# All 71 matmuls on constants that stand in TensorE's pauses are taken out of a two-block conv and FFN kernel

## The chip, the cores and the metric

One core of one Trainium2 chip. The metric is the device time of one execution in microseconds (us), the median of several runs. The hardware profiler gives one execution's trace besides: what each engine ran and when, and the clock that TensorE was granted.

## The reference, cut to what matters

The input is x, 4 images of 32 channels and 28 x 28 points. Four blocks with a residual follow one another. The norm ahead of each, `ln_c` or `ln_t`, is over the 32 channels of a point, since the tokens are the points.

```python
x = x + L0_conv(ln_c(x))          # 1x1 conv, L1-distance conv (adder2d) 1x1, BN, relu,
                                  # 3x3 conv, adder2d 3x3, BN, relu, + identity, relu
t = to_tokens(x)                  # (4, 784, 32)
t = t + L0_ffn(ln_t(t), ...)      # scan over 33 steps, see below
x = from_tokens(t, x)
x = x + L1_conv(ln_c(x), ...)     # two 3x3 convs with quantised weights and activations
t = to_tokens(x)
t = t + L1_ffn(ln_t(t), ...)      # causal convolution with 16 filters, mixed by 32x32 matrices
x = from_tokens(t, x)

def step(h, p):                   # L0_ffn, scanned over 33 sets of weights
    op = argmax(h[0, 0, :19])     # the first token chooses one of 19 operations
    y = softmax(q k^T * scale) v @ p['wo'][op]      # q, k, v = h @ p['wq'][op], ...
    h = where(p['am'][op], y, h)  # attention only where the mask says so
    z = relu(h @ p['w1'][op] + p['b1'][op]) @ p['w2'][op] + p['b2'][op]
    h = where(p['fm'][op], z, h)
    return h, None
```

## The kernel before

Each engine has its own instruction stream, written out by hand, and they meet by semaphores alone. Partitions hold 4 images x 32 channels, the 784 points lie along the free dimension, in halves of 392 (`half`) or quarters of 196 (`quarter`). Everything is float32 except the quantised convs. A float32 matmul call shows in the trace as two matmul instructions, each with its weight load. All of TensorE's matmuls go through the helper `mm`, so they carry one line, L879, and are told apart by the tiles they read.

The order of the work on TensorE:

1. `norm(0)`: the mean over channels of each point by a matmul of X with the constant `bones` (two halves, on tiles X,CON), DVE subtracts it, ACT squares, a matmul with `vsel` sums the squares (TMP,CON), ACT takes the root (SDC), DVE the reciprocal (RSC), and `spread` (four calls, RSC,CON) copies the result to all channels; DVE multiplies. The same `norm` runs four times (k = 0 to 3).
2. 1x1 conv (XN,WS), the correction with `CORRN` (QZ,CORRN), and 8 adder groups. In an adder group ACT or DVE makes one plane of |x - w| or max(x, w) of the whole batch (L338, L365, L534, L729), and TensorE sums it over channels in 8 calls (`group`, pool_,CON).
3. 3x3 conv (H1P,WS) and 72 more adder groups; `norm(1)`.
4. The scan. `token_row` brings the first token's row to partition 0; DVE finds the operation and the next step whose mask is set (`decide`), writes it to KINT (semaphore `decided`), and every engine reads it and jumps in three nested loops (`active_steps`). SP fetches the step's weights, DVE lays them out in blocks (W1B, W4B), and then attention (projection H,W4B; scores QZ,Y; `weigh` multiplies the exponentials with VT and with ones) and FFN (H,W1B, then W2S) run where the step asks for them. With this input two steps run: the first has FFN alone, the second attention and FFN. Then the row is read a third time, nothing is left, and all engines leave the loops.
5. `norm(2)`, two quantised 3x3 convs (H1P,CQ, bf16), `norm(3)`, short matmuls with shifted copies (CW,MUB and CON,CW), and the filter bank: 64 `filtered` and 16 `mixed` blocks on HE and pool_, dense up to the end.

Between these stand calls of `keep_warm(n)`: n matmuls of constants with constants (CON with itself, 128 x 196 columns; in `inputs` the tile XC, part of TMP, which DVE has just set to zero) into a PSUM bank that nobody reads at that point. The numbers are in `WARM`. They stand: `inputs` ahead of everything; `means` in each norm after the two mean matmuls; `deviations` in each norm after vsel; `choice` after each token row; `weights` at the head of each step; `exponentials` before the last image's four `weigh`; `sums` before the wait for the last of the weighed sums. Nothing waits for them.

Of the kernel before, what the change touches and what calls it, by code (L numbers as in the profile page):

```python
# [22 lines left out]
P = 128  # L23
NIMG, C, SIDE = 4, 32, 28
T = SIDE * SIDE
QU = T // 4
# [4 lines left out]
NB, NOPS, HID = 33, 19, 128  # L31
STEPS = (3, 4, 3)

WARM = dict(inputs=4, means=1, deviations=4, choice=8, weights=8, exponentials=5, sums=2)
OPW = 1024
QT, NQ = 112, 7
NK = 16
# [31 lines left out]
@contextmanager  # L69
def active_steps(e, code):  # L70


    assert STEPS[0] * STEPS[1] * STEPS[2] >= NB
    with e.Fori(0, STEPS[0]):
        with e.If(e.snap(code, min_val=0, max_val=4 * NB + 7) > 0):
            with e.Fori(0, STEPS[1]):
                with e.If(e.snap(code, min_val=0, max_val=4 * NB + 7) > 0):
                    with e.Fori(0, STEPS[2]):
                        c = e.snap(code, min_val=0, max_val=4 * NB + 7)
                        with e.If(c > 0):  # L80
                            yield c
                        e.nop()
                e.nop()
        e.nop()


def build(nc, x, par, con, ws1, wa1c, wa1r, ws2, wa2c, wa2r, amt, fmt, fwa, fwb, aw,
          cw1, cw2, phe, pho, mpp, mpm, mu, out):
    with ExitStack() as ctx:
# [11 lines left out]
        XC, SQ, SD, RS = (TMP[:, n * T:n * T + T] for n in range(4))  # L101
# [46 lines left out]
        def con_(name, w=None, rows=P):  # L148
            a = CC[name]
            return CON[0:rows, a:a + (w or P)]  # L150
# [4 lines left out]
        def half(ap, h):  # L155
            return ap[:, h * HT:(h + 1) * HT]

        def quarter(ap, q):
            return ap[:, q * QU:(q + 1) * QU]
# [6 lines left out]
        def bank(b, w=HT, rows_=slice(0, P)):  # L166
            return PS[rows_, b, 0:w]
# [709 lines left out]
        def _(t):  # L877
            def mm(out_, lhsT, rhs, start=True, stop=True):
                return t.matmul(out_, lhsT, rhs, start=start, stop=stop, skip_group_check=True)  # L879

            def keep_warm(n, src=CON, b=3):

                for _ in range(n):
                    mm(bank(b, QU), src[:, 0:P], src[:, 0:QU])

            def spread(h, to):

                for q in (2 * h, 2 * h + 1):
                    last = mm(PS[:, to + h, QU * (q % 2):QU * (q % 2) + QU], con_("spread", 512)[:, P * q:P * q + P], RSC[:, :])
                return last  # L890

            def norm(k, src, ready=None):
                for h in range(2):
                    if k == 0:
                        t.wait_ge(s["x_low_in" if h else "x_in"], 16)
                    if ready:
                        t.wait_ge(s[ready], h + 1)
                    mm(bank(h), con_("bones"), half(src, h)).then_inc(s["ln_mean"], 1)
                keep_warm(WARM["means"])
                for q in range(4):  # L900
                    t.wait_ge(s["ln_sq"], 2 * k + q // 2 + 1)
                    last = mm(PS[32 * q:32 * q + 32, 2, 0:QU], con_("vsel", C), quarter(SQ, q))
                last.then_inc(s["ln_var"], 1)
                keep_warm(WARM["deviations"])
                t.wait_ge(s["ln_rs"], k + 1)
                for h in range(2):
                    spread(h, 0).then_inc(s["ln_bc"], 1)

            t.wait_ge(s["idle_src"], 1)
            keep_warm(WARM["inputs"], XC)  # L910
            t.wait_ge(s["con_head"], 16)
            norm(0, X)
            t.wait_ge(s["ws_rep"], 1)
            for h in range(2):
# [52 lines left out]
            for h in range(2):  # L967
                last = mm(bank(6 + h), con_("ident"), half(XS9, h), False, False)
            last.then_inc(s["adder_done"], 1)
            norm(1, X1, "x1_ready")  # L970
            t.wait_ge(s["ln_out"], 4)

            def token_row():
                mm(PS[0:1, 6, 0:32], H[:, 0:1], con_("ident", 32)).then_inc(s["row_done"], 1)
                keep_warm(WARM["choice"])

            token_row()
            t.wait_ge(s["decided"], 1)
            code = t.alloc_register("t_code"); na = t.alloc_register("t_na"); nf = t.alloc_register("t_nf")
# [3 lines left out]
            chosen = t.alloc_register("t_chosen")  # L983
            t.reg_mov(chosen, 1)
            with active_steps(t, code) as c:
                keep_warm(WARM["weights"])
                with t.If((c & 1) > 0):
                    k = t.snap(na, min_val=0, max_val=NB)
                    t.wait_ge(s["zeroed"], 4)
# [44 lines left out]
                    def weigh(b, pair):  # L1034

                        t.wait_ge(s["exp_done"], k * 28 + (NQ * b + min(2 * pair + 2, NQ)))
                        if pair == 0:
                            if b:
                                t.wait_ge(s["ae_done"], k * 4 + b)
                            else:  # L1040
                                t.wait_ge(s["v_done"], k + 1)
                        for h in range(2):
                            for w in range(2):
                                for e in range(2):
                                    j = 2 * pair + e
                                    if j < NQ:
                                        q = 64 * w + 32 * e
                                        last = mm(PS[q:q + 32, 6 + h, 0:HT],
                                                  con_("ones", C, QT) if w else VT[0:QT, j, 32 * b:32 * b + 32],
                                                  half(SCR[0:QT, NQ * (b % 2) + j, :], h), pair == 0, j + 2 >= NQ)  # L1050
                        last.then_inc(s["pv_done"], 1)
# [16 lines left out]
                    weigh(NIMG - 2, 2)  # L1068
                    maxima_spread(NIMG - 1)
                    weigh(NIMG - 2, 3)  # L1070
                    keep_warm(WARM["exponentials"], b=0)
                    for pair in range(4):
                        weigh(NIMG - 1, pair)
                    t.wait_ge(s["wo_diag"], k + 1)
                    keep_warm(WARM["sums"], b=0)
                    t.wait_ge(s["ae_done"], k * 4 + 4)
                    for b in range(NIMG):
                        for q in range(4):
# [12 lines left out]
                with t.If((c & 2) > 0):  # L1091
# [18 lines left out]
                    t.wait_ge(s["ffn_h"], k * 2 + 2)  # L1110
                    t.reg_add(nf, nf, 1)
                token_row()
                n = t.snap(chosen, min_val=1, max_val=NB)
                t.wait_ge(s["decided"], n + 1)
# [4 lines left out]
            n = t.snap(chosen, min_val=1, max_val=NB + 1)  # L1119
            t.wait_ge(s["x2_ready"], n)  # L1120
            norm(2, X)
            t.wait_ge(s["cq_done"], 2)
            for i, (w, src) in enumerate(((CQ1, XQP), (CQ2, HQP))):
# [177 lines left out]
```

## Time and profile before

| | |
|---|---|
| median of 3 runs | 438.93 us (436.95 to 442.23) |
| the profiled execution | 438.08 us, span of its instructions 436.3 us |
| mean granted clock of TensorE | 0.98 of full speed |
| TensorE matmuls busy | 395.4 us, 91%, 4974 instructions |
| DVE busy | 244.8 us, 56% |
| ACT busy | 185.9 us, 43% |
| GpSimd busy | 17.3 us, 4% |

The span is from the first to the last instruction; the execution's time is 1.8 us longer. Matmuls are pipelined and their ends are modelled, so a group of n matmuls lasts about (n - 1) starts' spacing and one latency. "Issue" is idle time of an engine in which it waited for nothing that the profile shows, for example while its sequencer jumps. The granted clock is in shares of 2.4 GHz; 0.50 is 1.2 GHz.

### The profile page before, as it was taken

The numbers are of one execution on the slowest core, as the hardware profiler recorded it, in microseconds if no ns is written. First come the engines' busy times: TensorE is split into PE (matmuls) and PEld (weight loads), VectorE is DVE, ScalarE is ACT, GpSimd is POOL, SyncE is SP. The second block draws the span as 40 slices with busy tenths as digits, with TensorE's granted clock in tenths as the row PEclk, the third lists the DMA queues.
The fourth block names the chain that finished last, engine by engine and source line by source line (L and its number), as shares of the span: only waits on it lengthen the run. The fifth ranks groups of instructions, "written<-read, shape, count | busy, mean of one in ns | idle before, by whom it ended". The sixth has DMA issues, their size and how long they took to land.

```text
span 436.3 us, 11302 instructions
## 1 busy us (share of the span) xinstructions
PE 395.4 (91%) x4974; PEld 228.1 (52%) x4974; DVE 244.8 (56%) x337; ACT 185.9 (43%) x179; POOL 17.3 (4%) x30
## 2 busy tenths in 40 slices
PE   6899999999999898799989889866799999999996
PEld 4436357633333374656353534434377666777774
DVE  1797899999999455565747495434621121212121
ACT  2554888878787113144737366322221111111110
POOL 3054000000000200000000000000000000000000
PEclk9899999999999989999999999998989999999999
DMA  4139000000000250000000000000000000000001
GB/s 141 23 82 374 27 2 2 2 3 2 2 2 2 86 213 10 15 0 0 2 0 2 0 2 2 0 2 0 0 2 2 3 3 5 4 3 3 3 3 40
DMA packets 9768, 11.58 MB, mean 27 GB/s; under 512 B 3894, under 2 KB 8888, under 8 KB 9720
## 3 DMA queue, kind: packets, MB, share of 16 engines
q1 hardware_dynamic: 9352, 9.55, 6.7%
q0 software_dynamic: 224, 1.10, 0.8%
q8 instruction: 41, 0.67, 0.6%
q10 hardware_dynamic: 144, 0.20, 0.1%
q14 instruction: 7, 0.06, 0.0%
HBM read 10.44 MB, written 0.40 MB: 25 GB/s over the span
## 4 chain that ended last, share of the span: by engine, by line
PE 72%; DVE 14%; issue 6%; ACT 3%; DMA 2%; SPq 1%; DVEq 1%; ACTq 0%
PE PS L879 72%; DVE pool_ L788 3%; DVE pool_ L729 3%; DVE TMP L800 1%; ACT pool_ L393 1%; DMA PAR<-in_par 1%; DVE RSC L497 1%; ACT pool_ L409 1%; DMA W4R<-in_aw 1%; SPq L212 1%; ACT TMP L397 0%; DVE TMP L842 0%; DVE TMP L843 0%; DVE CW L686 0%; DVE SMX L805 0%
## 5 line engine op out<-in xcount | busy, mean ns | idle before, releaser
L879 PE MATMUL PS<-pool_,CON 128*32 128x392 f32 (+1 forms) x1392 | 132.3, 497 | 1.1 <-DVE pool_ L729 1.0
L879 PEld LDWEIGHTS PS<-pool_,CON 128*32 128x32 f32 (+1 forms) x1392 | 54.2, 111 | 60.2 <-issue 45.1
L365 ACT ACTIVATE pool_<-TMP,WA 128x3136 f32<-128x3136 f32 x27 | 78.5, 2929 | 16.6 <-PE PS L879 16.3
L729 DVE TENSOR_SCALAR pool_<-TMP,WA 128x3136 f32<-128x3136 f32 x45 | 82.0, 1847 | 0.2
L868 DVE COPY pool_<-PS 128x392 f32<-128x392 f32 x32 | 18.1, 566 | 84.0 <-PE PS L879 84.0
L463 ACT ACTIVATE pool_<-PS 128x392 f32<-128x392 f32 x32 | 15.9, 497 | 85.8 <-PE PS L879 85.8
L879 PE MATMUL PS<-pool_,WS 128*32 128x136 f32 (+3 forms) x1024 | 46.3, 333 | 0.0
L879 PE MATMUL PS<-HE,WS 128*32 128x136 f32 (+3 forms) x1024 | 46.3, 333 | 0.0
L879 PEld LDWEIGHTS PS<-pool_,WS 128*32 128x32 f32 x1024 | 32.0, 110 | 14.8 <-issue 9.8
L879 PEld LDWEIGHTS PS<-HE,WS 128*32 128x32 f32 x1024 | 31.5, 111 | 15.5 <-issue 11.2
L879 PE MATMUL PS<-QZ,Y 128*112 128x392 f32 x112 | 39.4, 498 | 0.0
L393 ACT ACTIVATE pool_<-pool_ 112x784 f32<-112x784 f32 x28 | 23.3, 853 | 17.2 <-DVE pool_ L788 17.2
L409 ACT ACTIVATE pool_<-PS 112x784 f32<-112x784 f32 x28 | 22.8, 814 | 16.4 <-PE PS L879 16.4
L879 PE MATMUL PS<-pool_,VT 112*32 112x392 f32 x112 | 23.9, 498 | 6.3 <-ACT pool_ L393 6.2
L788 DVE TENSOR_TENSOR pool_<-pool_,PS 112x784 f32<-112x784 f32 x28 | 26.5, 964 | 5.2 <-PE PS L879 5.2
L879 PE MATMUL PS<-CON 128*128 128x196 f32 x136 | 28.1, 354 | 0.2 <-issue 0.2
L879 PEld LDWEIGHTS PS<-QZ,Y 128*112 128x112 f32 x112 | 18.6, 176 | 17.0 <-issue 12.9
L879 PEld LDWEIGHTS PS<-CON 128*128 128x128 f32 x136 | 24.1, 202 | 6.3 <-issue 5.7
L800 DVE TENSOR_TENSOR TMP<-TMP,pool_ 112x784 f32<-112x784 f32 x20 | 19.5, 973 | 5.7 <-ACT pool_ L409 5.7
L879 PE MATMUL PS<-X,CON 128*128 128x392 f32 (+1 forms) x24 | 10.2, 596 | 9.3 <-issue 4.3
L879 PEld LDWEIGHTS PS<-pool_,VT 112*32 112x32 f32 x112 | 6.0, 109 | 21.3 <-ACT pool_ L393 14.4
L879 PE MATMUL PS<-pool_,ASEG 128*32 128x49 f32 (+2 forms) x512 | 14.4, 248 | 0.1
(204 smaller groups left out, 337.7 us busy)
## 6 DMA issues: line engine op xcount, KB each, us to landing
pool_<-in_pho SPq DMA_DIRECT2D x1, 3144.0 KB, 10.6
HE<-in_phe SPq DMA_DIRECT2D x1, 3136.0 KB, 14.1
CW<-in_cw SPq DMA_DIRECT2D x2, 576.0 KB, 4.3
CON<-in_con POOLq DMA_DIRECT2D x1, 732.5 KB, 6.3
out_y<-Y SPq DMA_DIRECT2D x1, 392.0 KB, 2.4
CON<-in_con POOLq DMA_DIRECT2D x1, 337.0 KB, 3.6
CQ<-in_ws SPq DMA_DIRECT2D x16, 9.0 KB
MPP<-in_mpp SPq DMA_DIRECT2D x1, 256.0 KB, 2.6
```

The costliest lines, as they stand in the source:

```text
L212: sp.dma_start(PAR[q, 0:PC["cb"]], rows_).then_inc(s["par_in"], 16)
L365: a.activation(RING[:, g % RG, :, :].rearrange("p b (r c) -> p b r c", r=SIDE), window(n // CQ), ACT.Abs, bias=WA2[:, n:n + 1], scale=-1.0 ...
L393: a.activation(tile, tile, ACT.Exp, scale=SCALE).then_inc(s["exp_done"], 1)
L409: a.activation(SCR[0:QT, NQ * (b % 2) + j, :].rearrange("p (h t) -> p h t", h=2), PS[0:QT, pr:pr + 2, 0:HT], ACT.Copy).then_inc(s["score_c ...
L463: a.activation(UEV[:, u % 8, :], bank(u % 6), ACT.Copy).then_inc(s["uev_act"], 1)
L497: v.reciprocal(RSC[:, :], SDC[:, :]).then_inc(s["ln_rs"], 1)
L729: v.tensor_scalar(RING[:, g % RG, :, :].rearrange("p b (r c) -> p b r c", r=SIDE), window(n // CQ), WA2[:, n:n + 1], None, ALU.max).then_i ...
L788: v.tensor_tensor(tile, tile, PS[0:QT, 4:6, 0:HT], ALU.add).then_inc(s["less_max"], 1)
L800: v.tensor_tensor(TOP[0:QT, :], before, SCR[0:QT, NQ * (b % 2) + j, :], ALU.max).then_inc(s["top_step"], 1)
L868: v.tensor_copy(UEV[:, u % 8, :], bank(u % 6)).then_inc(s["uev_dve"], 1)
L879: return t.matmul(out_, lhsT, rhs, start=start, stop=stop, skip_group_check=True)
```

## The change

The table WARM, the helper `keep_warm` and its seven calls in the text are deleted; in this run they made 71 calls. The order of everything else, all waits and all buffers stay as they are.

```diff
-WARM = dict(inputs=4, means=1, deviations=4, choice=8, weights=8, exponentials=5, sums=2)
...
-            def keep_warm(n, src=CON, b=3):
-
-                for _ in range(n):
-                    mm(bank(b, QU), src[:, 0:P], src[:, 0:QU])
-
...
                     mm(bank(h), con_("bones"), half(src, h)).then_inc(s["ln_mean"], 1)
-                keep_warm(WARM["means"])
                 for q in range(4):
...
                 last.then_inc(s["ln_var"], 1)
-                keep_warm(WARM["deviations"])
                 t.wait_ge(s["ln_rs"], k + 1)
...
             t.wait_ge(s["idle_src"], 1)
-            keep_warm(WARM["inputs"], XC)
             t.wait_ge(s["con_head"], 16)
...
                 mm(PS[0:1, 6, 0:32], H[:, 0:1], con_("ident", 32)).then_inc(s["row_done"], 1)
-                keep_warm(WARM["choice"])
...
             with active_steps(t, code) as c:
-                keep_warm(WARM["weights"])
                 with t.If((c & 1) > 0):
...
                     weigh(NIMG - 2, 3)
-                    keep_warm(WARM["exponentials"], b=0)
                     for pair in range(4):
                         weigh(NIMG - 1, pair)
                     t.wait_ge(s["wo_diag"], k + 1)
-                    keep_warm(WARM["sums"], b=0)
                     t.wait_ge(s["ae_done"], k * 4 + 4)
```

## Rows read from the trace of the kernel before

**Rows 1.** The page: busy time by engine, and the granted clock in 40 slices.

```profile
PE 395.4 (91%) x4974; PEld 228.1 (52%) x4974; DVE 244.8 (56%) x337; ACT 185.9 (43%) x179; POOL 17.3 (4%) x30
...
PEclk9899999999999989999999999998989999999999
```

**Rows 2.** Groups by line and shape: count | busy us, mean ns | idle before.

```profile
L879 PE MATMUL PS<-CON 128*128 128x196 f32 x134 | 27.9, 357 | 0.2 <-issue 0.2
...
L879 PE MATMUL PS<-TMP 128*128 128x196 f32 x8 | 3.0, 554 | 1.1 <-DVE TMP L511 1.1
```

**Rows 3.** Stretches: from:to, length, busy PE, PEld, DVE, ACT, POOL, PEclk, DMA, GB/s.

```profile
19.43:22.84 3.41, 3.41 (x24) 0.79 (x20) 3.41 (x3) 3.41 (x2) 0.00 (x0) 0.50 0.11 18
148.80:152.55 3.75, 1.67 (x4) 0.78 (x5) 2.74 (x5) 1.41 (x3) 2.64 (x3) 1.00 0.63 234
...
180.70:183.27 2.57, 0.62 (x3) 0.47 (x3) 1.20 (x6) 0.00 (x0) 0.00 (x0) 1.00 0.23 45
...
219.00:222.80 3.80, 2.25 (x14) 1.30 (x12) 1.92 (x3) 0.88 (x2) 0.00 (x0) 1.00 0.00 0
295.91:299.32 3.41, 3.41 (x10) 1.54 (x8) 1.12 (x2) 0.96 (x2) 0.00 (x0) 0.50 0.00 0
312.97:316.39 3.42, 1.46 (x4) 0.69 (x5) 3.23 (x7) 0.65 (x1) 0.00 (x0) 1.00 0.00 0
```

**Rows 4.** Timeline of PE at the start: start us, length us, what [idle before <-releaser].

```profile
1.14 2.98 PE L879 MATMUL PS<-TMP 128*128 128x196 f32 x8 [1.14 <-DVE TMP L511]
4.87 2.98 PE L879 MATMUL PS<-X,CON 128*128 128x392 f32 x4 [0.76 <-DMA CON<-in_con]
7.65 0.86 PE L879 MATMUL PS<-CON 128*128 128x196 f32 x2
10.82 1.00 PE L879 MATMUL PS<-TMP,CON 128*32 128x196 f32 x8 [2.31 <-ACT TMP L316]
...
13.75 1.59 PE L879 MATMUL PS<-RSC,CON 128*128 128x196 f32 x8 [0.41 <-DVE RSC L497]
15.43 1.60 PE L879 MATMUL PS<-XN,WS 32*128 32x392 f32 x16
18.45 1.93 PE L879 MATMUL PS<-QZ,CORRN 32*32 32x392 f32 x16 [1.43 <-issue]
```

**Rows 5.** Timeline of PE from norm(1) to the first FFN.

```profile
150.73 0.93 PE L879 MATMUL PS<-X,CON 128*128 128x392 f32 x2 [1.97 <-DVE X L735]
...
153.37 1.50 PE L879 MATMUL PS<-TMP,CON 128*32 128x196 f32 x8
...
159.05 0.22 PE L879 MATMUL PS<-CON,H 128*1 128x32 f32 x2 [0.66 <-DVE H L500]
...
166.96 5.53 PE L879 MATMUL PS<-H,W1B 128*128 128x392 f32 x16 [1.68 <-DVE W1B L823]
```

**Rows 6.** Timeline of PE at the head of the second step.

```profile
175.14 5.57 PE L879 MATMUL PS<-CON 128*128 128x196 f32 x32
182.66 4.59 PE L879 MATMUL PS<-H,W4B 128*128 128x392 f32 x8 [1.95 <-DVE W4B L773]
```

**Rows 7.** Timeline of PE around the block ahead of the last weighing.

```profile
265.07 1.93 PE L879 MATMUL PS<-CON 128*128 128x196 f32 x10
267.55 0.52 PE L879 MATMUL PS<-pool_,VT 112*32 112x392 f32 x2 [0.56 <-ACT pool_ L393]
```

**Rows 8.** Timelines of DVE, ACT and PE from the last decision to the convs.

```profile
289.19 0.14 DVE L749 CAST KINT<-KMAX 1x1 int32<-1x1 f32 x1
...
293.73 1.28 ACT L441 ACT_TABLE_LOAD   x1 [6.61 <-issue]
...
288.31 2.92 PE L879 MATMUL PS<-CON 128*128 128x196 f32 x16
295.58 2.68 PE L879 MATMUL PS<-X,CON 128*128 128x392 f32 x4 [4.34 <-issue]
...
305.41 3.25 PE L879 MATMUL PS<-H1P,CQ 128*128 128x392 bf16 x18 [1.88 <-DVE H1P L849]
```

## Prediction, made before the changed kernel was run

> **What bounds the kernel now.** I read the page first [rows 1]: TensorE (PE) is busy 91% of the span, and the line of its granted clock has a digit under 9 in four slices only. So PE sets the end in its dense stretches (the adder groups up to 148.8 us, the filter bank from 331.5 us), and hand-overs between PE, DVE and ACT set it in the thin ones between. Then the groups by line and shape, for what the filler is [rows 2]: 134 matmul instructions on CON and 8 on the zeroed TMP, two to a call, so 71 calls: 4 inputs, 4 x 1 means, 4 x 4 deviations, 3 x 8 choice, 2 x 8 weights, 5 exponentials, 2 sums (the loop ran two steps, three rows were read, one step had attention). Their 27.9 + 3.0 us of busy time is the most that could come back. Then the stretches, for the clock [rows 3]: it stood at 0.50 (1.2 GHz) in five stretches of 3.41 us, beginning at 19.43, 152.55, 183.27, 295.91 and 316.39 (two are shown). The column also says 1.00 at the start, but the instructions there run at the low level: the 8 of TMP at 1.14 took 2.98 us, 8 of the same shape on RSC at 13.75 took 1.59, and the filler at 7.65 is slow too, 0.86 us for two [rows 4]. Last the timelines around each filler, for what it holds up and what it covers.
>
> **What the filler holds up: nearly nothing.** Inputs end at 4.12 us (1.14 + 2.98); the first real matmul waits until 4.87 for CON to land [rows 4]. Choice and weights run while DVE decides and the weights are fetched: the first pair ends long before FFN's first matmul at 166.96, which DVE's copy of the loaded weights released [rows 5]; the second pair ends at 180.71 and attention's projection starts at 182.66, again behind DVE's copy [rows 6]. The exponentials block ends at 267.00, the next weighing starts at 267.55, released by ACT [rows 7]. Means and deviations stand under ACT's squares and root and DVE's reciprocal; where vsel starts after a means block, its second half waits for ACT's second square anyway. Sums stand under ACT's copy of the last weighed sums. So I count 0 gained. The one doubt is the last choice block: it ends at 288.31 + 2.92 = 291.23, and norm(2) starts 4.34 us later, booked to issue, while ACT, leaving the same loop, went on at 293.73 [rows 8]. If PE's sequencer began to leave the loop only when the filler was out, 291.23 - 289.33 = 1.9 us would come back (the decision fell at 289.19 + 0.14). Against it: in the second pair 32 filler instructions run without a gap over the turn of the loop [rows 6], so the sequencer runs ahead of the array. I take 0, bound -1.9.
>
> **What the filler covers: the clock.** Work at 1.2 GHz takes twice as long, so a slow stretch of 3.41 us on the path costs 1.7. Before it fell at 152.55 PE had been busy 1.67 of 3.75 us, before 183.27 for 0.62 of 2.57, before 316.39 for 1.46 of 3.42; over 219.0 to 222.8, with 2.25 of 3.80, it did not fall [rows 3]. The pauses of PE before the falls were short: 1.97 us at 150.73 [rows 5], 1.95 at 182.66 [rows 6].
> The Trainium skill ("TensorE: Matmul & The Clock Gate", section "Why this matters for your kernels") asks for an idle gap of more than about 3 us before the clock is lost in mid-kernel. The trace does not agree: two falls came behind pauses of 2 us. By that rule the sum below would be that of rival (a), 3.3 us, instead of 10.1.
> How long is a restart slow? After 4.34 us of idle PE was slow from 295.58 to 299.32 (the first 0.33 us apart). At the start it was still slow at 7.65 and fast at 10.82, so from 4.87 at least 3.6 and at most 5.9 us; from its very first instruction at 1.14 at most 9.7, at least 7.4 [rows 4, 8]. I take 3.8 us, so 1.9 lost where PE is the path, and 3.7 (7.4 us) as the upper bound, 1.7 as the lower. In order of time:
>
> 1. Start. Without inputs and means PE has only the four X matmuls (2.98 us) before a pause, so I expect it still slow as norm(0) goes on. Slow costs: vsel 1.50 instead of 1.00, +0.5 [rows 4, 5]; spread 2.98 instead of 1.59, +1.4; the first conv's 1.60, +1.1; CORRN's 1.93, in part slow already, +1.0 [rows 4]. All of it is 4.0. But the fall at 19.43 (1.7 us) need not come on top: if the clock rises in the spread and holds, it is 0.5 + 0.7 - 1.7 = -0.5. I take 2.2.
> 2. norm(1). Before, the fall at 152.55 was over at 155.96, ahead of the spread, with deviations filling PE in between. Without them PE idles between vsel and spread: spread slow, +1.4, or 0 if it did not fall; 1.2.
> 3. First FFN. PE now idles from the token row's end at 159.27 to 166.96, 7.7 us, where two blocks stood. Its H,W1B matmuls take 5.53 us at full speed, on the path [rows 5]. A restart: 1.7 to 3.7; 1.9.
> 4. Second step. Before already paid a slow stretch from 183.27, 0.6 us after the projection began [rows 6]. Now it begins slow at once: +0.3, from 0 to 2.0 (3.7 - 1.7).
> 5. Exponentials. 265.07 to 267.55 becomes a pause of 2.5 us ahead of some 5.5 us of weighing [rows 7]. A fall would cost up to 1.7; a little under one in two: 0.8.
> 6. norm(2) and the quantised convs. The restart at 295.58 is slow as before. Before, filler and vsel kept PE full from 298.05 to 301.52 and the clock was back at 299.32. Now vsel +0.3, spread +1.4, and a slow stretch into the convs (the first 18 instructions took 3.25 us), up to +1.7 [rows 8]. 3.4 if all comes, 0 if it rises as before; 2.0.
> 7. norm(3) and what follows. Before, the stretch from 316.39 was over at 319.80, ahead of the spread. Without deviations again: spread +1.4, then up to 1.7 in the dense short matmuls behind it; 3.1 at most, 0 at least; 1.7.
>
> The adder groups and the filter bank hold no filler and keep their speed. Sum: 2.2 + 1.2 + 1.9 + 0.3 + 0.8 + 2.0 + 1.7 = 10.1 us. The profiled execution took 438.1 us (span 436.3), 0.85 us under the median 438.93 of the runs. So 448.2, rounded to 448. Lower ends: -0.5 + 0 + 1.7 + 0 + 0 + 0 + 0 = 1.2, 439.3 us (437.4 with the -1.9); upper ends: 4.0 + 1.4 + 3.7 + 2.0 + 1.7 + 3.4 + 3.1 = 19.3, 457.4 us.
>
> **Rivals.** (a) Only long pauses cost. The falls at 152.55, 183.27 and 316.39 came in spite of filler, so both kernels have them; new are the restart of the first FFN (1.9) and a slow spread at the start (1.4): 441.4 us. For it: the pauses inside attention brought no fall (219.0 to 222.8). Against: the falls behind 2 us. Chance 0.17. (b) Not slower: the slow stretches stay five, since filler did not prevent those, and PE leaves the loop 1.9 us sooner, at the idle ahead of 295.58; it decides if the clock's new losses stay under 1.9. 436.2 us. Against: the first FFN can hardly start fast after 7.7 us of idle. Chance 0.05. (c) Through the thin stretches the clock stays low, since short bursts never bring it back: near the sum of the upper ends, 455 us. For it: at the start PE was busy 2.98 us (on zeros) and again from 4.87, and was slow for 7.4 us [rows 4]. Against: each later stretch ended after 3.41 us, though all of those were full. Chance 0.16. My forecast, 448 us (445 to 452), has 0.62.
>
> **How the numbers follow.** A measurement of this kernel can tell about 1% from no change (its three runs lie from 436.95 to 442.23), 4.4 us, so slower begins at 443.3. Forecast and (c) are slower, 0.78, and so is a part of (a), whose time moves by 2 us with where the falls land, 0.04: slower 0.82. The rest of (a) and 0.02 of (b) are the same, 0.15; faster has what is left of (b), 0.03. The range leaves out (b), the low half of (a) and the upper third of (c): 441 to 455.
>
> **What would show it.** Stretches at 0.50 should rise from five to eight or more, the mean clock fall under 0.96; H,W1B of the first FFN should take 7 to 8 us instead of 5.53 (step 3); the spreads of norm(1) and norm(3) near 2.9 us instead of 1.59 (steps 2, 7); the filter bank should be unchanged. If FFN's first matmuls run at full speed, the whole picture is wrong. If norm(2) starts 6.2 us after the decision as before, nothing was gained at the loop's end. If the slow stretches stay five, (a) or (b) holds.

## The result

The changed kernel took 455.67 us in the median (451.99 to 460.71, four runs) against 439.16 us for the kernel before: ratio 1.034, 95% interval 1.024 to 1.045. Run once more beside other variants it took 455.28 us (451.70 to 457.09) against 438.48, ratio 1.036 (1.030 to 1.042). So taking the filler out costs some 16 us (15.1 and 15.8 by the ratios, 16.5 and 16.8 by the medians), and nothing of it comes back anywhere. The ratios leave out executions over 1.5% above their kernel's fastest, and the first profiled execution of the changed kernel was one (460.71 us), so the lines below are those of the repetition, whose profiled execution took 456.90 us; before is the kernel of [rows 1 to 8].

The page of the changed kernel, repeated: busy time and the granted clock in 40 slices.

```profile
PE 384.1 (84%) x4832; PEld 214.4 (47%) x4832; DVE 244.8 (54%) x337; ACT 186.0 (41%) x179; POOL 18.4 (4%) x30
...
PEclk9689999999999966689999998975867999999999
```

The 142 instructions are gone (4974 to 4832), PE is busy 11 us less, and the span is 18.7 us longer. DVE and ACT did the same work in the same time. The clock line [rows 1] has lost its nines where the kernel is thin: at the start, in the scan's first half, once at the last weighing, and from the exit of the scan to the filter bank. The same in stretches (from:to, length, busy PE, PEld, DVE, ACT, POOL, PEclk, DMA, GB/s):

```profile
11.40:18.20 6.80, 4.86 (x22) 3.68 (x24) 2.59 (x4) 0.58 (x2) 0.00 (x0) 0.50 0.13 29
...
152.60:158.20 5.60, 2.90 (x12) 0.88 (x12) 3.46 (x5) 1.48 (x3) 0.82 (x1) 1.00 1.05 387
158.20:161.60 3.40, 2.98 (x8) 2.46 (x8) 0.89 (x3) 0.00 (x0) 0.00 (x0) 0.50 0.78 277
...
165.00:178.60 13.60, 7.76 (x12) 3.75 (x13) 4.97 (x12) 2.92 (x4) 0.00 (x0) 0.50 0.05 10
...
185.50:195.70 10.20, 5.01 (x8) 2.80 (x9) 3.93 (x11) 2.76 (x3) 0.00 (x0) 0.50 0.06 15
273.95:276.37 2.42, 0.01 (x1) 0.00 (x1) 2.42 (x4) 2.37 (x4) 0.00 (x0) 1.00 0.04 7
277.60:281.00 3.40, 3.40 (x24) 0.99 (x24) 1.21 (x2) 2.45 (x4) 0.00 (x0) 0.50 0.00 0
301.50:322.00 20.50, 12.12 (x34) 6.02 (x35) 6.37 (x13) 3.65 (x6) 0.00 (x0) 0.50 0.00 0
...
332.20:345.90 13.70, 11.10 (x43) 9.91 (x44) 2.51 (x3) 1.48 (x3) 0.00 (x0) 0.50 0.01 1
350.20:451.20 101.00, 100.85 (x2561) 70.52 (x2560) 18.13 (x33) 15.91 (x32) 0.00 (x0) 1.00 0.01 3
```

Eight slow stretches instead of five [rows 3]. What matters more is their length: before each was 3.41 us, now they last 3.4, 6.8, 10.2, 13.6, 13.7 and 20.5 us, about 75 us together instead of 17. (The first profiled execution has seven, also 75 us together.) Not all of that is lost work: TensorE was idle in a part of them, as from 165.00 to 169.84. The mean clock is 0.917 instead of 0.98. The filter bank runs at full speed as before.

The timeline of PE in the same execution (start, length, what, idle before), for the places of [rows 4 to 8]:

```profile
13.38 2.98 PE L878 MATMUL PS<-RSC,CON 128*128 128x196 f32 x8 [1.94 <-DVE RSC L496]
16.29 2.53 PE L878 MATMUL PS<-XN,WS 32*128 32x392 f32 x16
...
158.31 2.98 PE L878 MATMUL PS<-RSC,CON 128*128 128x196 f32 x8 [1.94 <-DVE RSC L496]
...
169.84 1.67 PE L878 MATMUL PS<-H,W1B 128*128 128x392 f32 x2 [7.68 <-DVE W1B L822]
172.51 7.89 PE L878 MATMUL PS<-H,W1B 128*128 128x392 f32 x14 [0.99 <-issue]
...
190.69 5.37 PE L878 MATMUL PS<-H,W4B 128*128 128x392 f32 x8 [7.58 <-DVE W4B L772]
...
305.65 2.97 PE L878 MATMUL PS<-X,CON 128*128 128x392 f32 x4 [6.99 <-issue]
...
312.64 2.98 PE L878 MATMUL PS<-RSC,CON 128*128 128x196 f32 x8 [1.94 <-DVE RSC L496]
317.51 6.37 PE L878 MATMUL PS<-H1P,CQ 128*128 128x392 bf16 x24 [1.88 <-DVE H1P L848]
...
335.01 2.98 PE L878 MATMUL PS<-RSC,CON 128*128 128x196 f32 x8 [1.94 <-DVE RSC L496]
338.64 6.17 PE L878 MATMUL PS<-CW,MUB 128*128 128x49 f32 x24 [0.66 <-DVE CW L499]
```

Every spread of a norm takes 2.98 us instead of 1.59, the first FFN's H,W1B from 169.84 to 180.40, 10.56 us instead of 5.53. The ledger by stage, the first from the start of the span and each other from the start of one DVE instruction to the start of the next; the numbers are the profiled executions' differences to before, in us. The two columns on the right belong to the first two experiments.

| step of the prediction | ends with DVE's | before, start | predicted | changed, repeated | scan filler back | norm filler back |
|---|---|---|---|---|---|---|
| 1 start and adders | second TMP<-TMP,XN of norm(1) | 150.59 | 2.2 | 1.90 | 3.00 | 3.14 |
| 2 norm(1), choice | first W1B copy | 166.69 | 1.2 | 0.98 | 0.95 | 0.27 |
| 3 first FFN | last H of the first step | 174.23 | 1.9 | 5.03 | 0.00 | 2.72 |
| 4 second step's head | first QZ copy (L780) | 188.30 | 0.3 | 0.89 | -0.06 | 0.32 |
| 5 attention, second FFN | last X<-X,H | 289.43 | 0.8 | 1.47 | 1.43 | 1.51 |
| 6 norm(2), convs | first TMP (L857) after the convs | 312.98 | 2.0 | 3.93 | 3.66 | 0.38 |
| 7 norm(3) to the filter bank | first copy of the filter bank | 334.58 | 1.7 | 4.52 | 3.83 | -0.60 |
| sum | | | 10.1 | 18.72 | 12.81 | 7.74 |

### The profile page after: what moved, and what is told of

Read it like the earlier page. It is cut to its first block, busy times and chain, and to the rows that moved or that the text cites. A ratio compares the mean times of both kernels' runs of the same rounds, so it can differ in the third digit from the quotient of the medians.

```text
span 458.9 us, 11019 instructions
## 1 busy us (share of the span) xinstructions
PE 385.5 (84%) x4832; PEld 217.5 (47%) x4832; DVE 248.2 (54%) x337; ACT 186.0 (41%) x179; POOL 14.0 (3%) x30
## 4 chain that ended last, share of the span: by engine, by line
PE 59%; DVE 26%; issue 8%; ACT 4%; DMA 2%; SPq 1%; DVEq 1%; ACTq 0%
PE PS L878 59%; DVE pool_ L728 9%; DVE pool_ L787 3%; DVE pool_ L533 2%; DVE TMP L799 1%; DVE RSC L496 1%; DMA PAR<-in_par 1%; ACT pool_ L392 1%; ACT pool_ L408 1%; DMA W4R<-in_aw 1%; SPq L211 1%; DVE TMP L494 1%; ACT TMP L315 0%; ACT SDC L317 0%; ACT TMP L396 0%
## 5 line engine op out<-in xcount | busy, mean ns | idle before, releaser
L878 PE MATMUL PS<-pool_,CON 128*32 128x392 f32 (+1 forms) x1392 | 134.1, 501 | 3.1 <-DVE pool_ L533 2.2
L878 PEld LDWEIGHTS PS<-pool_,WS 128*32 128x32 f32 x1024 | 34.0, 110 | 12.8 <-issue 5.4
L878 PEld LDWEIGHTS PS<-HE,WS 128*32 128x32 f32 x1024 | 33.4, 111 | 13.7 <-issue 5.9
L878 PE MATMUL PS<-pool_,VT 112*32 112x392 f32 x112 | 25.3, 532 | 8.2 <-ACT pool_ L392 8.1
L408 ACT ACTIVATE pool_<-PS 112x784 f32<-112x784 f32 x28 | 22.8, 815 | 16.4 <-PE PS L878 16.4
L878 PE MATMUL PS<-H,W1B 128*128 128x392 f32 x32 | 14.5, 611 | 9.8 <-DVE W1B L822 8.9
L878 PE MATMUL PS<-RSC,CON 128*128 128x196 f32 x40 | 12.7, 487 | 7.9 <-DVE RSC L496 7.7
L878 PEld LDWEIGHTS PS<-RSC,CON 128*128 128x128 f32 x40 | 10.3, 282 | 11.1 <-DVE RSC L496 10.2
## 6 DMA issues: line engine op xcount, KB each, us to landing
HE<-in_phe SPq DMA_DIRECT2D x1, 3136.0 KB, 15.1
```

The source lines that it names most:

```text
L408: a.activation(SCR[0:QT, NQ * (b % 2) + j, :].rearrange("p (h t) -> p h t", h=2), PS[0:QT, pr:pr + 2, 0:HT], ACT.Copy).then_inc(s["score_c ...
```

## The experiments

The theory: the filler does nothing but keep PE's clock up. Its rivals: that the instructions in PE's queue matter and not the work of the array; that the loss comes from races between engines that the new timing at the start tips over; and, for single blocks, that they are worth nothing.

**The scan's filler back alone (e1_scan).**

```diff
-WARM = dict(inputs=4, means=1, deviations=4, choice=8, weights=8, exponentials=5, sums=2)
+WARM = dict(inputs=0, means=0, deviations=0, choice=8, weights=8, exponentials=0, sums=0)
```

> The changed kernel with the filler of the scan put back (choice=8, weights=8), everything else out. Clock theory, by the shifts between the two traces (H,W1B of the first FFN 5.53 us before, 10.0 us from first start to last end after; projection 4.59 against 5.14): those 4.3 + 0.5 us come back, so about 451 us, and the first FFN's 16 matmuls take 5.5 to 6 us again, although they still start behind DVE's copy. Rival, that the late start of everything (races between engines at the beginning) made the loss: nothing comes back but noise, 454 to 457 us.

Measured: 450.38 us (448.04 to 450.96), ratio to before 1.019 (1.013 to 1.026). PE's timeline in the first step:

```profile
163.16 2.92 PE L879 MATMUL PS<-CON 128*128 128x196 f32 x16
166.31 2.91 PE L879 MATMUL PS<-CON 128*128 128x196 f32 x16 [0.24 <-issue]
170.91 5.53 PE L879 MATMUL PS<-H,W1B 128*128 128x392 f32 x16 [1.68 <-DVE W1B L823]
```

The FFN is at full speed again, and the ledger's steps 3 and 4 are back at 0; steps 6 and 7 stay. So the scan's filler is worth 5 us of the 16, all of it in what follows directly behind it. Races at the start would have left the time where it was, so they are not what these 5 us are.

**The norms' filler back alone (e2_norms).** The same line with means=1, deviations=4 and the others 0.

> The changed kernel with the filler in the norms put back (means=1, deviations=4), inputs, scan and attention blocks out. Clock theory: the spreads of norm(0), norm(1) and norm(3) take 1.6 us again instead of 3.0, and the convs and the short matmuls behind norm(3) run at full speed for the larger part; from the shifts (norm(1) 1.7, norm(2) with its convs 3.2, norm(3) with what follows 3.8, start 2 of 3.1) about 9 us come back at most: 446 to 449 us. The first FFN stays slow (9 to 10 us). If norm filler is worth nothing because each norm begins at the low clock anyway: 454 us or more.

Measured: 443.58 us (441.00 to 445.83, ten runs), ratio 1.007 (1.004 to 1.010). PE's timeline from norm(1) to the first FFN:

```profile
158.20 1.88 PE L879 MATMUL PS<-CON 128*128 128x196 f32 x8
160.21 1.59 PE L879 MATMUL PS<-RSC,CON 128*128 128x196 f32 x8
...
170.37 8.26 PE L879 MATMUL PS<-H,W1B 128*128 128x392 f32 x16 [7.69 <-DVE W1B L823]
```

More comes back than I expected, 12 us. The spread is at 1.59 us, and steps 6 and 7 of the ledger are gone, although this kernel comes out of the scan as cold as the other (no choice filler): five filler calls in the norm, some 1.8 us of work at full speed (an estimate from 2.91 us for 8), join the restart into one piece. The clock is up at 309.01, 5.7 us after norm(2) began at 303.27 and before the convs at 313.75; in e1_scan, with no filler in the norm, it was up only 15.8 us after (300.67 to 316.51). This is the block worth most. The spread of norm(0) is fast only in part (2.28 us). The first FFN stays slow, but costs 2.7 us and not 5.0.

**The filler as one column each (e3_onecol).**

```diff
-                    mm(bank(b, QU), src[:, 0:P], src[:, 0:QU])
+                    mm(PS[0:1, b, 0:1], src[:, 0:1], src[:, 0:1])
```

> The kernel before with every filler call kept in place and number, but shrunk to one column of one stationary column, so it issues the same 142 matmul and 142 weight-load instructions and leaves the array idle. The output does not depend on filler. Clock theory: as the changed kernel, 452 to 458 us, slow stretches as many as there. Rival, that it is the instructions in the queue that matter (sequencer kept running, no restart): 437 to 441 us.

Measured: 457.14 us in the median, ratio 1.034 (1.026 to 1.043), mean clock 0.921. From the page (span and busy time) and the groups by line and shape:

```profile
span 456.0 us, 11302 instructions
...
L879 PE MATMUL PS<-RSC,CON 128*128 128x196 f32 x40 | 13.1, 497 | 7.9 <-DVE RSC L497 7.7 <-DVE RSC L812 0.2
...
L879 PE MATMUL PS<-CON 128*1 128x1 f32 x136 | 5.7, 164 | 4.8 <-issue 4.8
```

All 11302 instructions of before are there, and the time is that of the changed kernel; the spreads are slow (497 ns a matmul, 342 before). It is the work of the array that holds the clock, not the instructions. The rival of the queue is out.

**GpSimd's memsets moved (e4_pool).** In the first profiled execution of the changed kernel one of DVE's five L533 planes took long. That line's instructions there (durations min/median/max in ns):

```profile
L533 DVE TENSOR_SCALAR pool_<-QZ,WA x5: 1834/1846/4929, 21.5 to 33.6; 128x3136 f32<-128x3136 f32 x5
```

GpSimd's timeline in the same execution:

```profile
26.86 2.18 POOL L287 COPY WS<-CQ 128x128 f32<-128x128 f32 x9 [16.36 <-DMA CQ<-in_ws]
28.98 0.52 POOL L289 MEMSET W1B<- 128x512 f32 x1
29.44 0.52 POOL L290 MEMSET W4B<- 128x512 f32 x1
29.91 1.37 POOL L291 MEMSET MUB<- 128x1536 f32 x1
31.23 0.79 POOL L296 MEMSET TMP<- 128x120 f32 x4
```

The long plane began at 28.73 and ended 4.93 us later, 1.64 us after GpSimd's last memset (32.02), as if it had run only then.

```diff
-            g.memset(W1B[:, :, :], 0.0).then_inc(s["zeroed"], 1)
-            g.memset(W4B[:, :, :], 0.0).then_inc(s["zeroed"], 1)
-            g.memset(MUB[:, :, :], 0.0).then_inc(s["zeroed"], 1)
...
+            g.wait_ge(s["adder_done"], 1)
             for e in (edge[:, :, 0, :], edge[:, :, PS_ - 1, :], edge[:, :, 1:1 + SIDE, 0], edge[:, :, 1:1 + SIDE, PS_ - 1]):
                 g.memset(e, 0.0).then_inc(s["pads"], 1)
-            g.wait_ge(s["adder_done"], 1)
+            g.memset(W1B[:, :, :], 0.0).then_inc(s["zeroed"], 1)
+            g.memset(W4B[:, :, :], 0.0).then_inc(s["zeroed"], 1)
+            g.memset(MUB[:, :, :], 0.0).then_inc(s["zeroed"], 1)
```

> The changed kernel with GpSimd's memsets of W1B, W4B, MUB and of the edges moved behind the first adder_done, so that they no longer run while DVE makes the last planes of the first eight adder groups. In the profile of the changed kernel one of DVE's L533 took 4.93 us instead of 1.85, ending with GpSimd's last memset. If that stall comes from sharing with GpSimd, no L533 takes over 3 us here and 1 to 3 us come back: 453 to 455 us. If the long one has another cause, it stays and so does the time, 455.7 us.

Measured: 455.19 us (454.18 to 456.90), ratio 1.033 (1.026 to 1.040). The long plane is gone:

```profile
L532 DVE TENSOR_SCALAR pool_<-QZ,WA x5: 1848/1854/1953, 21.1 to 30.0; 128x3136 f32<-128x3136 f32 x5
```

But the time does not tell it from the changed kernel's 455.67 and 455.28, whose executions have the long plane only sometimes (the repetition had none, the one-column kernel of e3_onecol had it too, 4.93 us). So this is a part of single executions, up to 3 us, and not of the 16 us.

**The weights block alone (e5_weights).** The line with weights=8 and the others 0.

> The changed kernel with only the weights block put back: 8 filler calls (2.6 us of work at full speed) at the head of each step, ending 1.7 to 2 us ahead of the first real matmul, after 3 to 5 us of idle. With choice and weights both back the first FFN ran at full speed and the time was 450.4 us. If the clock needs only something shortly before the work, this gives the same, 450 to 451 us. If 2.6 us behind an idle array are too little to bring it up, the first FFN stays slow (8 to 10 us for H,W1B) and the time is 453 to 456 us.

Measured: 450.07 us (448.02 to 450.91), ratio 1.028 (1.022 to 1.034). Choice and weights together gave 450.38 us and 1.019 (1.013 to 1.026): the same time, but beside a kernel before of 440.13 us where this one had 437.78, and the two intervals overlap. PE in the first step:

```profile
166.25 4.71 PE L879 MATMUL PS<-CON 128*128 128x196 f32 x16 [3.09 <-issue]
170.85 5.53 PE L879 MATMUL PS<-H,W1B 128*128 128x392 f32 x16
```

The block begins slow, so its 8 calls last 4.71 us instead of 2.91, right up to the FFN, and bring the clock up in that time. Slow filler stretches itself into the gap. The second step gains too: at the first FFN's end this kernel is 3.88 us behind before, at DVE's first QZ copy only 2.45, because the projection now runs at full speed, which it did not in before (183.27, [rows 3]). And the clock did not fall at the last weighing, though the exponentials block is out (step 5 of the ledger 0.08). So no gain of the choice blocks shows, and by the ratios one of a few us can't be excluded; the first FFN, though, has its 5.53 us either way. The calls that count there stand right ahead of the work.

**Exponentials and sums out of the kernel before (e6_noexp).** The line of before with exponentials=0 and sums=0.

> The kernel before with only the exponentials and sums blocks taken out. Clock theory, from the profile of the changed kernel: the pause of 2.4 us ahead of the last weighing brings a slow stretch in most executions, +1.4 us in the profile, so a median 0.8 to 1.5 us over before; in an execution without that stretch nothing. Rival: the stretch was chance, 0 us.

Measured: 439.91 us against 437.78, ratio 1.0033 (1.0004 to 1.0062), by the ratio 1.4 us, with 0.2 to 2.7 in the interval. Stretches of it, and PE at the end of the pause:

```profile
262.00:269.10 7.10, 4.68 (x40) 2.41 (x40) 5.27 (x6) 4.62 (x7) 0.00 (x0) 1.00 0.00 0
269.10:272.60 3.50, 3.50 (x28) 1.18 (x28) 0.99 (x2) 2.23 (x3) 0.00 (x0) 0.51 0.00 0
...
267.65 0.52 PE L879 MATMUL PS<-pool_,VT 112*32 112x392 f32 x2 [2.42 <-ACT pool_ L393]
```

One slow stretch behind the pause, in the middle of the weighing, as in the changed kernel (277.60 there).

**More filler in the scan (e7_choice).** The line of before with choice=20 and weights=3.

> The kernel before with more filler in the scan: choice 20 calls instead of 8, weights 3 instead of 8. 23 calls take 7.5 us, which just fills the 7.5 to 7.7 us from the token row to the first real matmul of each step, and 20 calls (6.5 us) the exit from the loops (7.3 us). Clock theory: the slow stretches at the second step's projection and at norm(2) go, up to 1.7 us each on the path: 436 to 438 us against 439 to 440 for before. Rival: filler that long holds up PE's sequencer or the real work: 440 us or more, with PE's first real matmul of a step later than the copy that releases it.

Measured: 444.02 us (442.66 to 445.55), ratio 1.013 (1.008 to 1.018): 1.3% slower. DVE's copy and PE in the first step:

```profile
167.90 0.97 DVE L823 COPY W1B<-W1R 32x128 f32<-32x128 f32 x4 [0.99 <-DMA W1R<-in_fwa]
...
170.82 7.22 PE L879 MATMUL PS<-H,W1B 128*128 128x392 f32 x16 [2.51 <-issue]
```

The FFN starts 2.9 us after the copy, where before it was 0.27 us [rows 5], and PE is idle for issue. I read this as its sequencer held up by the long block, with the branch still ahead; the sequencer's own times are not in the rows. The idle time also cost clock: it fell at 171.86, and the FFN took 7.22 us instead of 5.53. The same at the exit: norm(2) starts at 302.18, 8.9 us after the decision (293.30), instead of 6.2, and the slow stretch there is 6.8 us long instead of 3.4. Of the two that I expected to go, only the one at the projection went. Holding the clock up and holding the sequencer up are two ends of one block.

**The same with filler around the norms (e8_filled).**

```diff
             def norm(k, src, ready=None):
+                keep_warm((0, 6, 0, 4)[k])
                 for h in range(2):
+                    if h:
+                        keep_warm((0, 1, 0, 3)[k])
...
                     spread(h, 0).then_inc(s["ln_bc"], 1)
+                keep_warm((0, 2, 5, 2)[k])
```

> As the kernel with 20 choice calls, and besides filler ahead of norm(1) (6 calls) and norm(3) (4), between their halves (1 and 3) and behind the spreads of norm(1), norm(2) and norm(3) (2, 5 and 2). Clock theory: the slow stretches at norm(1) and norm(3) go too; two of at most 1.7 us: 433 to 436 us, with a mean clock of 0.99. Rival, that filler beyond the present amount delays work as much as it saves: 438 us or more.

Measured: 443.55 us (440.38 to 444.78), ratio 1.011 (1.006 to 1.016). The slow stretch at norm(2) is gone (those at norm(1) and norm(3) were missing in the profile of e7_choice already), the hold-up of the long blocks stays, and so does the slow stretch in the first FFN (172.38).

**choice=8, weights=12 and the norms' extra filler (e9_weights12), and with GpSimd's memsets moved besides (e10_w12_pool).**

The line of before with weights=12, and norm calls as in the diff above; the second with the diff of e4_pool besides.

> The kernel before with the filler of the norms extended as in the kernel with 20 choice calls and more in the norms, but with choice at its old 8 and weights at 12 instead of 8, so that no block is longer than PE's queue can take while its sequencer goes on. Clock theory: no slow stretch at the second projection (1.7), at norm(1) (about 1) and at norm(3) (0.6 of the path), the one at the exit from the loops stays: 434 to 437 us against 438 to 440 for before. If 12 calls still hold up the branch behind them, the first H,W1B starts more than 0.5 us after DVE's copy and the time is 439 us or more.

> The same with GpSimd's memsets of W1B, W4B, MUB and of the edges behind the first adder_done. In before these already run mostly behind the first groups, so nothing to 0.5 us: 434 to 437 us.

Measured: 438.49 us and 438.51 us against 438.48; ratios 1.0006 (0.997 to 1.004) and 0.9985 (0.996 to 1.001). No gain. The clock line on the page of the first (e9_weights12):

```profile
PEclk9989999999999999999999999997999999999999
```

PE's timeline in the first step of the second (e10_w12_pool):

```profile
162.08 4.24 PE L878 MATMUL PS<-CON 128*128 128x196 f32 x24 [0.36 <-issue]
167.40 5.53 PE L878 MATMUL PS<-H,W1B 128*128 128x392 f32 x16 [1.08 <-DVE W1B L822]
```

The slow stretches at norm(1), at the projection and at norm(3) are gone as expected, but already 12 calls make the FFN start 1.1 us behind the copy (at 166.28), and in the other 1.4. By the ledger the second step's head gives back 1.7 us (e9_weights12) and 1.4 (e10_w12_pool), and the late FFN takes 1.2 and 0.8: much of what the clock gave, the sequencer took. The two profiles' spans are 0.5 us longer and 1.1 us shorter than before. Extra filler in the norms with weights left at 8 was not run.

**The changed kernel again (e11_after), and with three more memsets on GpSimd (e12_pool_more).**

```diff
+            for n in range(3):
+                g.memset(MUB[:, :, :], 0.0).then_inc(s["again"], 1)
+                g.wait_ge(s["again"], n + 1)
             g.memset(MUB[:, :, :], 0.0).then_inc(s["zeroed"], 1)
```

> The changed kernel itself once more, beside the other variants on one chip: 452 to 457 us. To see whether the 4.9 us plane of DVE's L533 comes in every execution: if its place depends on when GpSimd's copies meet DVE's last two planes, it comes in this profile too, as in the one with one-column filler, and not where the first conv is 0.3 us earlier.

> The changed kernel with three more memsets of MUB (1.37 us each) on GpSimd ahead of the one that is there, 4.1 us of work that nobody waits for before the second conv. If a plane of DVE waits while GpSimd works (one port between them), the long L533 grows from 4.9 to as much as 9 us where it waited before, and the time by up to 4 us, to 456 to 460. If the two engines only slow each other a little, or DVE holds GpSimd off, the planes stay at 1.85 us or 4.9, GpSimd ends later and the time stays at 452 to 457 us.

Measured: 455.28 us, and 458.48 us (453.08 to 461.72; ratio 1.040, 1.032 to 1.048). In both profiled executions DVE's planes are short and it is GpSimd that is held off, its nine copies taking 6.67 and 5.56 us instead of 2.18. GpSimd in the changed kernel, repeated:

```profile
26.44 6.67 POOL L287 COPY WS<-CQ 128x128 f32<-128x128 f32 x9 [17.21 <-DMA CQ<-in_ws]
```

So of DVE's plane and GpSimd's copies one waits for the other. In twelve of the fourteen profiles of this case a copy or memset of GpSimd waited for a plane (1.84 us for a copy of 0.29). In the other two, the first of the changed kernel and e3_onecol, the plane waited; in both it began beside GpSimd's last copy, with the memsets next. In the changed kernel's first profile it began 1.87 us after the first copy (28.73 and 26.86); in e4_pool it began 1.64 us after, and the ninth copy waited. So a few tenths of a microsecond decide; by what rule was not tested. A price of more memsets does not show: the intervals overlap (1.030 to 1.042 for the repetition), and no plane was long. One shorter operation of DVE (H<-KEYT) took 1.71 us instead of 0.47 there, beside a memset of 1.37.

## Why the prediction was right or wrong

**What bounds, and what the filler holds up.** Right. Nothing came back: in the ledger no stage of the changed kernel is faster. The doubt about the exit is settled: norm(2) starts 305.65 - 299.60 = 6.05 us after the decision without filler and 6.25 with it [rows 8], so the 8 calls held nothing up, and the -1.9 was rightly left out. Over all profiles it is 6.0 to 6.3 us with 8 calls at the exit and 6.0 to 6.1 without. But only for blocks of this length: 12 calls cost 0.8 to 1.1 us (1.1 and 1.4, less the 0.27 of [rows 5]), 20 cost 2.6 (2.9 - 0.27).

**That the clock is the whole price.** Right: the one-column filler gives the changed kernel's time. The parts roughly add up: scan 455.3 - 450.4 = 4.9, norms 455.3 - 443.6 = 11.7, exponentials 1.4, together 18.0 for 16.8. The kernel before had medians from 437.8 to 440.1 us beside these runs, so they can't tell 18.0 from 16.8. The inputs block was never tried alone.

**The size.** Too low: 10.1 us by the sum, 15 to 17 measured, and 448 against 455.3 and 455.7, past the range that I thought likely (445 to 452) and at the upper end of the wide one (441 to 455). Adding the sum to the profiled execution and not to the median, 0.85 us higher, made it lower still. The direction and the list of places were right, and the likeliest case was not the one that came; the time is that of rival (c). The term that was mis-sized is the length of a restart, "I take 3.8 us". In the profiled executions without choice and weights filler the first FFN, starting after 7.7 us of idle (in e3_onecol with one-column calls in them), stayed slow for 4.6 us (e3_onecol, 175.18 to 179.8), 5.5 (e2_norms, 170.37 to 175.9), 6.3 (e4_pool), 7.4 (the changed kernel's first), 8.7 (e12_pool_more) and 8.8 (169.84 to 178.60 above). I had measured a restart where filler stood behind it: 295.58 to 299.32 [rows 8] was short because of the filler this change removes. The same restart took 15.8 us in e1_scan, which lacks only the norms' filler there. The upper bound, 7.4 us, came from the start, and the range of step 3 went by it.

- Step 1: 1.90 for 2.2, near, but in part by luck. The spread (2.98 us for 1.59) and the first conv (2.53 for 1.60) were slow as said; vsel was not (1.00, where I had put 1.50), CORRN took less than before (1.52 for 1.93), and the kernels with less filler lost 1.9 to 3.2 us there, 6.8 and 7.0 in the two profiles with the long plane. Step 2: 0.98 for 1.2; right.
- Step 3: 5.03 for 1.9, over its upper bound of 3.7. Of it 4.0 us are the slow restart, and 0.99 are an idle time for issue between the second and third matmul, which the list of costs did not have.
- Step 4: 0.89 for 0.3, in its range. Step 5: 1.47 for 0.8; I gave the fall a little under one in two, and it came in eight of the nine profiles without that block at work (not in e5_weights).
- Step 6: 3.93 for 2.0, over the 3.4 that "if all comes" gave. All came: the stretch 301.50 to 322.00 is 20.5 us long, with PE busy 12.12 of them, in bursts of about 1 to 6 us, and 16.4 us of it lie behind the start of norm(2). Before, the means and deviations joined the bursts of the norm into one, and the clock was up 3.7 us after that start.
- Step 7: 4.52 for 1.7, over 3.1. The same: 332.20 to 345.90, though PE was busy 11.10 of 13.70 us. The 24 matmuls on CW,MUB took 6.17 us instead of 3.32, a loss for which I had left 1.7.

Of the signs, the eight stretches, the mean clock under 0.96, the slow spreads, the unchanged filter bank and norm(2) at 6 us after the decision came; the first FFN's 10.56 us is far over the 7 to 8 that I had named.

**The rivals.** (a), only long pauses cost: out. The clock fell at 158.20 with no pause over 1.97 us in the 5.6 us before, and e6_noexp loses 1.4 us to a pause of 2.4. Even in the kernel before, the fall at 316.39 [rows 3] had only pauses of 1.16 and 0.87 us in the 3.4 us before it:

```profile
314.06 0.93 PE L879 MATMUL PS<-X,CON 128*128 128x392 f32 x2 [1.16 <-DVE X L858]
315.86 1.19 PE L879 MATMUL PS<-X,CON 128*128 128x392 f32 x2 [0.87 <-DVE X L858]
```

The Trainium skill ("TensorE: Matmul & The Clock Gate", section "Why this matters for your kernels") advises no idle gap over about 3 us between bursts. That is not enough here; the traces have falls after pauses of 1.2, 1.9 and 2.4 us. (b) is out. (c), that short bursts never bring the clock back, came near: they do, but the low stretches last 10 to 20 us. I had given it 0.16, with "all of those were full" against it; that every later stretch was full was the work of the filler, and so no evidence on a kernel without it.

## What to carry to other kernels

Where TensorE works in short bursts, filler matmuls ahead of and between them are worth taking seriously: here they cost no measurable time and gave some 16 us, most of it from five calls in each norm. Put them right ahead of the real work and inside the run of bursts, not at the beginning of a long pause, where no gain showed; a block that starts at the low clock stretches to fill the gap. Keep a block short where a branch stands behind it: 8 calls were free, 12 cost about 1 us and 20 cost 2.6. And when pricing a removal, don't read the length of a slow stretch from a place that the removed thing itself made short.

## What the runs showed of the hardware

- The granted clock can stay at 1.2 GHz for 20.5 us while TensorE is busy 12.12 of them, and for 13.7 us with 11.10 busy. From the start of norm(2) it was low for 16.4 us with the norm's bursts apart (15.8 in e1_scan), and for 3.7 (before) and 5.7 us (e2_norms) with filler between them.
- The clock can fall behind pauses of TensorE of 1.16 and 0.87 us (before, at 316.39), and does not always fall behind one of 2.42 us (e5_weights).
- A float32 plane of DVE (TENSOR_SCALAR, 1.85 us) and copies and memsets of GpSimd exclude each other: the plane took 4.93 us in one order, GpSimd's nine copies 6.67 us instead of 2.18 in the other. DVE's TENSOR_TENSOR of 0.80 us and a memset of 0.52 ran side by side at their usual lengths (the changed kernel, repeated, at 33.0).
- After 7.7 us of idle TensorE stopped for 0.31 to 1.17 us for issue behind the second matmul of the first FFN, in four of the five profiles with no filler at all in the scan (not in e2_norms); the cause is open.
- TensorE takes a block of 32 instructions of filler (8 calls) without delay; with 48 (12 calls) the real work behind the branch came 0.8 to 1.1 us later than before after the copy that it needs, with 80 (20 calls) 2.6 us later.
